# One opening block, later constants made inside the first attention, and call lists of their own for the passes without an output stage

## What is computed

```python
# layer 0, with shift/scale/gate vectors from silu(c0) @ wmod0 (6 x 256 per sample)
h = _layernorm(x) * (1 + scale_a) + shift_a
x = x + gate_a * attention(h)        # 16 heads of 16, causal, layer-normed q and k, exact softmax
h = _layernorm(x) * (1 + scale_b) + shift_b
u = silu(h @ w1.T * s1) * (h @ w2.T * s2)
u = gelu(u @ h1.T * sh1); u = gelu(u @ h2.T * sh2)
x = x + gate_b * (u @ w3.T * s3)
# layer 1, with vectors from silu(c1) @ wmod1
x = x + gate_a * selective_scan_block(h)   # in_proj, dt/B/C projection, scan over 512 steps, 16 states
x = x + gate_b * (mx_quantize(h) @ mx_quantize(weight).T + bias)
```

## Time and profile before

| | us |
|---|---|
| median of 3 runs | 4080.57 (4078.65 to 4083.61) |
| profiled execution, its own time | 4077.96 |
| its span in the trace | 4076.2 |
| TensorE busy | 3502.1 (86%) |
| VectorE busy | 3318.9 (81%) |
| ScalarE busy | 2577.2 (63%) |
| GpSimd busy | 2721.2 (67%) |

### The profile page before, as it was taken

How to read it: one execution, slowest core, us unless ns; L and a number is a source line. 1 busy time by engine, 2 the same in 40 slices (tenths; PEclk the granted TensorE clock), 3 DMA queues, 4 the chain that set the end, 5 groups by cost and what they waited for, 6 DMA issues and landing times. The chain is left out here.

```text
span 4076.2 us, 49893 instructions
## 1 busy us (share of the span) xinstructions
PE 3502.1 (86%) x16757; PEld 2034.7 (50%) x16757; DVE 3318.9 (81%) x3665; ACT 2577.2 (63%) x3716; POOL 2721.2 (67%) x1957
## 2 busy tenths in 40 slices
PE   5488888989898998989897898989889898989876
PEld 3154553637355463736455373645546373644522
DVE  3513687989888898989887898988989898988997
ACT  2345666766676766766676676666667676667652
POOL 0031676958677685968766695877768696776892
PEclk9599999999999999999999999999999999999888
DMA  3520110303021020302112030301103030211100
GB/s 136 183 88 32 58 63 8 118 1 109 16 67 59 28 98 6 116 4 91 35 53 74 6 119 1 99 27 57 69 21 104 1 109 16 78 47 42 68 1 11
DMA packets 66249, 236.01 MB, mean 58 GB/s; under 512 B 9120, under 2 KB 9760, under 8 KB 65568
## 3 DMA queue, kind: packets, MB, share of 16 engines
q1 hardware_dynamic: 63648, 223.81, 16.3%
q10 hardware_dynamic: 2304, 8.39, 0.5%
HBM read 212.25 MB, written 19.92 MB: 57 GB/s over the span
## 5 line engine op out<-in xcount | busy, mean ns | idle before, releaser
L672 POOL TENSOR_TENSOR kept<-kept,hb 128x512 f32<-128x512 f32 x600 | 757.5, 1294 | 20.2 <-DVE hb L1989 19.6
L1980 DVE TENSOR_TENSOR_SCAN hb<-ps,hb 128x512 f32<-128x512 f32 x600 | 697.8, 1206 | 17.7 <-ACT ps L1404 13.1
L938 PE MATMUL ps<-hid_bhi,wring 128*128 128x512 f32 x1408 | 560.9, 398 | 16.0 <-DVE ln_s L2007 16.0
L938 PE MATMUL ps<-hid_blo,wring 128*128 128x512 f32 x1408 | 554.1, 394 | 0.0
L1404 ACT ACTIVATE ps<-kept,a_neg 128x512 f32<-128x512 f32 x600 | 403.3, 695 | 188.1 <-DVE hb L1980 188.1
L938 PE MATMUL ps<-hid_ahi,wring 128*128 128x512 f32 x1280 | 515.2, 402 | 4.9 <-DVE h_ln L2007 4.4
L633 POOL TENSOR_SCALAR_AFFINE_SELECT room<-room 128x512 f32<-128x512 f32 x256 | 224.3, 893 | 431.3 <-ACT room L1628 429.4
L938 PE MATMUL ps<-hid_alo,wring 128*128 128x512 f32 x1280 | 505.0, 395 | 0.0
L2055 DVE TENSOR_REDUCE room<-ps 128x4 f32<-128x2048 f32 (+3 forms) x256 | 375.1, 1486 | 118.1 <-PE ps L1132 118.1
L640 POOL TENSOR_TENSOR kept<-kept,hb 128x1024 f32<-128x1024 f32 x112 | 288.9, 2590 | 249.0 <-DVE hb L1924 181.1
L1628 ACT ACTIVATE room<-ps 128x2048 f32<-128x2048 f32 (+1 forms) x192 | 305.3, 1590 | 205.4 <-PE ps L1158 178.5
(11 more groups left out here) (319 smaller groups left out, 7680.1 us busy)
## 6 DMA issues: line engine op xcount, KB each, us to landing
wring<-w_hi SPq DMA_DIRECT2D x352, 512.0 KB, 3.3
kept<-in_wffn SPq DMA_DIRECT2D x22, 512.0 KB, 4.4
w_hi<-wring SPq DMA_DIRECT2D x22, 512.0 KB, 3.6
xn<-in_x_fm SPq DMA_DIRECT2D x17, 512.0 KB, 3.2
out_fm<-xc ACTq DMA_DIRECT2D x15, 512.0 KB, 2.7
room<-in_wmod SPq DMA_DIRECT2D x2, 1536.0 KB, 7.8
win<-in_win SPq DMA_DIRECT2D x1, 1024.0 KB, 8.7
wqk<-in_wqk SPq DMA_DIRECT2D x1, 512.0 KB, 5.7
```

What stands on the lines that cost most here:

```text
L672: pool.tensor_tensor(acc[:, m, :], acc[:, m, :], hb[:, s % 8, :], ALU.add).then_inc(acc_done, 1)
L938: mm = pe.matmul(bank(bk), w, x, start=(k == 0 and i == 0), stop=(k == K - 1 and i == 1))
L1980: dve.tensor_tensor_scan(hb[:, s % 8, :], bank(2 + m % 2), hb[:, s % 8, :], 0.0, ALU.mult, ALU.add).then_inc(scanned, 1)
```

## The change

- The setup block, the two memset blocks and the pass of number -1 become one block, `opening`. SP loads 16 tensors in it: the two c inputs, `mean_mat`, sample 0, the modulation matrix of layer 0, and what attention needs. The layer norm of sample 0 starts when its own two loads are there, and its variance product stands between the fourth and the fifth of the 12 groups of modulation products.
- The other 14 constants are loaded by SP in the first pass, one behind each stage load from tile 3 to tile 16. The modulation of layer 1 is made in the first pass (`later_pe`, `later_act`, `later_dve`). The quantisation of the last weight is made in the feed pass (`feed_dve`, `feed_pe`, `feed_act`).
- POOL, PE, ACT and DVE have a second list, for passes with `fin` false: the first pass, the feed pass and pass 1. For passes with `fin` true the lists are as they were, call for call. The second lists hold the same calls in another order, with the splitting steps at other places.

```diff
-        with nc.Block() as block:
-            n_set = len(SETUP_LOADS) + 10
...
+        def opening():
+            n_opening = 11
+
+            with nc.Block() as block:
+                @block.sync
+                def _(sp):
+                    sp.dma_start(c_in[:, 0, :], a["c0"]).then_inc(c_loaded, 16)
+                    sp.dma_start(c_in[:, 1, :], a["c1"]).then_inc(c_loaded, 16)
+                    sp.dma_start(whole(mean_mat), a["mean_mat"]).then_inc(x_loaded, 16)
+                    sp.dma_start(xn[:, :, :], a["x_fm"][0]).then_inc(x_loaded, 16)
+                    sp.dma_start(wm[0], a["wmod0"]).then_inc(mod_loaded, 16)
...
+                @block.scalar
+                def _(act):
+                    act.wait_ge(c_loaded, 32)
+                    act.activation(c_s, c_in, ACT.Silu).then_inc(set_act, 1)
+                    act.preload_act_table_set(LN_EXP)
+                    act.wait_ge(next_cent, 1)
+                    act.activation(qk_sq, ln_x[:, :, :], ACT.Square).then_inc(next_sq, 1)
...
+                    act.wait_ge(set_pe, 1)
+                    copy_modulation(act, 0, 0)
+                    act.wait_ge(next_norm, 1)
+                    act.wait_ge(set_dve, 2)
+                    for c in range(DC):
+                        act.activation(ln_x[:, c, :], ln_x[:, c, :], ACT.Identity, bias=mod[0][:, SA + c, 0:1],
+                                       scale=mod[0][:, CA + c, 0:1]).then_inc(att_in, 1)
...
+                @block.tensor
+                def _(pe):
+                    pe.wait_ge(x_loaded, 32)
+                    for c in range(DC):
+                        mm = pe.matmul(bank(6), mean_mat[:, :], xn[:, c, :], start=(c == 0), stop=(c == DC - 1))
+                    mm.then_inc(next_mean_done, 1)
+                    pe.wait_ge(mod_loaded, 16)
+                    pe.wait_ge(set_act, 1)
                     for m in range(6 * DC):
...
+                        mm = modulation(pe, 0, m, 0)
+                        if m == 3:
+                            pe.wait_ge(next_sq, 1)
+                            for c in range(DC):
+                                vv = pe.matmul(bank(7), mean_mat[:, :], qk_sq[:, c, :], start=(c == 0), stop=(c == DC - 1))
+                            vv.then_inc(next_var_done, 1)
...
+                @block.vector
+                def _(dve):
+                    dve.wait_ge(next_mean_done, 1)
+                    dve.tensor_tensor(ln_x[:, :, :], xn[:, :, :], bcast_c(bank(6)), ALU.subtract).then_inc(next_cent, 1)
+                    dve.wait_ge(next_rstd_ready, 1)
+                    dve.tensor_tensor(ln_x[:, :, :], ln_x[:, :, :], bcast_c(bank(7)), ALU.mult).then_inc(next_norm, 1)
+                    dve.wait_ge(set_act, 2)
+                    scales_of(dve, 0)
+                    gates_of(dve, 0, 2)
+
+                    dve.wait_ge(loaded, 16 * n_opening)
...
+        def later_pe(pe):
+            pe.wait_ge(loaded, 16 * N_LATER)
+            for m in range(6 * DC):
+                mm = modulation(pe, 1, m, 5)
+            mm.then_inc(set_pe, 1)
...
+        def feed_dve(dve):
+            for i in range(QN):
+                quant(dve, ffw, DC * D // QB, set_dve, 12, i)
...
                     sp.dma_start(stage[:, t % 3, :], a["wffn"][t]).then_inc(stage_loaded[t % 3], 16)
+                    if 3 <= t < 3 + N_LATER:
+                        to, name = LATER_LOADS[t - 3]
+                        sp.dma_start(to, a[name]).then_inc(loaded, 16)
...
+            if fin:
...
+            else:
+                split(0, 1)
+                square(0)
+                square(1)
...
-        run([Pass(-1, False, False, False, False, True, False, ())])
+        opening()
         turn_over()
         run([Pass(0, True, False, False, False, False, True, ())])
```

1946 lines of the change are left out of this document (1252 added, 694 removed).

## The result

The changed kernel took 4033.5 us in the median of 4 runs (4028.5 to 4041.4), the kernel before 4079.9 beside it: 0.9887 of its time, 95% interval 0.9872 to 0.9902. The forecast was 4024, the range 4004 to 4049. So the direction and the range held, and the gain is 46 us instead of 56. The profiled execution had a span of 4033.4 us (before 4076.2) in a run of 4035.1 us; between the two profiled executions the gain is 42.8 us.

A forecast was written before the change was run, and what follows sets the result against it. Before 453 us chains of waits bound the kernel, after that nearly full engines (DVE, PE). Opening -35.5, first pass -22, feed pass +5.1 and pass 1 -4 sum to -56.4, so 4024.2 us, range 4004 to 4049.

The forecast's parts named there:

- Opening, forecast -35.5: Opening: the first pass starts at 30.6 us instead of 66.1, a gain of 35.5 us.
- the 48 products: Opening: modulation matmuls on PE at the lower clock level, 16 in 3.4 us and 32 in 6.9.
- the result of -40: Opening: if sustained work raised the clock, some 4.5 us shorter, at -40; set aside in favour of the trace.
- the bound of -39: Opening: the largest gain allowed, -39 us, if the clock rises for the products.
- First pass, forecast -22: First pass: -28.4 us from reordered lists, +6.1 for the added modulation work; bounds -34 and -8.
- The walk: First pass: tile and attention chains stepped through from its start, putting scores_turned(2, 1) at 99.6 instead of 127.95, -28.4 us.
- the added loads: First pass: 14 loads, 3.8 MB, 9.5 us of transfer; the two large ones put at 0 cost.
- The rival with all 9.5: First pass: added loads queue ahead of the stage loads and take 9.5 us back, kernel at 4034; 12%.
- Feed pass, forecast +5.1: Feed pass: quantisation first on DVE delays the centring chain by 5.8 us, earlier rounding returns 0.7; bounds +4 and +7.
- Pass 1, forecast -4: Pass 1: an earlier exponential, and head-state work moved into an attention wait; -4 us, bounds -9 and +6.
- Steady passes, forecast 0: The 14 steady passes: lists kept, so no change unless the change does something to the clock.
- rival 4: Steady passes: a shifted start lowers the clock, each losing up to 3.7 us, 51 in all, kernel at 4075; 3%.

The follow-up runs named there:

- first_old: Changed kernel with its first pass running the kernel before's call lists, later constants ahead of scores(3,2), exp_probs(3,1) and weigh(3); 4062.1 us, 0.9962 of the kernel before.
- loads_late: Changed kernel with its 14 later loads issued behind the last tile instead of behind stage loads 3 to 16; 4036.1 us, 0.9896 of the kernel before.
- all_moved: Changed kernel joining quant_late, z_late, loads_late (wmod1 left early), opening_wqk, later_early and four extra opening matmuls on a zeroed tile; 4014.4 us, 0.9843.
- later_early: Changed kernel with later_pe's products in three parts, ahead of scores(1,1), scores(1,2) and scores(2,1) of the first pass; 4031.7 us, 0.9887 of the kernel before.
- quant_late: Changed kernel with VectorE's late weight quantisation moved from the feed pass's front to behind gate_up(7); 0.9883 of the kernel before.
- z_late: Changed kernel with two ScalarE calls exchanged in the new list, invert_sums(3) ahead of copy_z(0); 0.9883 of the kernel before.
- opening_wqk: Changed kernel with VectorE's preparation of wqk ahead of the scales and gates in the opening; 0.9885 of the kernel before.

## Why the prediction was right, and where it was off

**Opening, forecast -35.5, measured -37.6 in the profiled execution and -39 as a mean of nine traces.** The steps are the forecast's, and DVE's `wqk` preparation is the last as forecast. The term that was mis-sized is the 48 products, put at 10.3 us. I had taken the low level of the 96 products before for a property of such small matmuls and set aside the result of -40 with the clock raised. Nine traces show both: a start of 28.4 to 30.5 (-36 to -38) with the 32 products at 6.85 us, and of 24.4 to 25.6 (-41 to -42) with 3.7 to 4.2, past the bound of -39. Where all 48 products were at the lower level, the start (30.2 and 30.5 us) is the forecast's 30.6: the steps were right, and the gain beyond it is the clock's. The Trainium skill (TensorE: Matmul & The Clock Gate, Part 1: The HAM clock gate) says sustained work raises the clock; five traces of nine agree, in two the level rose and fell again ahead of the 32 products, and in two it stayed low through all 48.

**First pass, forecast -22, measured -15.6.** The walk was right in mechanism and nearly in size: first_old gives 27.8 for the lists, the walk 28.4. But its landmark `scores_turned(2, 1)` came at 104.0 and not 99.6. Of these 4.4 us the added loads, which I put at 0, are the likely 3: loads_late and all_moved show 3 in the tile chain, behind the 1 MB load, where I had counted 4 us of slack, and nothing behind the 1.5 MB load. The rival with all 9.5 was too large. The Trainium skill (DMA: Bandwidth & Descriptors, Queues, rings and completion order) says that on each DMA engine a queue's descriptors are consumed in ring order; the 7.3 us of tile 9's load against 3.4 in loads_late fit it. And `later_pe` was put at 5.5, since PE waits there anyway; it cost 7.0 to 7.3, and the pass's tail grew by 8.3 us instead of 6.1. Moved away, it leaves the pass some 6 us shorter (later_early).

**Feed pass, forecast +5.1, measured +6.1.** The step held as written; quant_late takes 6.8 of it back. Missing was that PE, idle for 6.83 us, went on mostly at its lower level (3.43 instead of 1.95).

**Pass 1, forecast -4, measured +1.2.** This step failed, in both halves. The moves that I counted happened. I had the second head state's scan shorten the second half, as the half where DVE is full; DVE's busy time there fell by 3.1 us and the half by 0.2 (114.76 to 114.57), so DVE's work did not set its length. In the attention half the last exponential came 108.1 us behind the start and not earlier than before (106.8), with PE busy 87.2 us instead of 80.8 for the same matmuls, at a granted clock of 0.87 against 0.94; in z_late, at 0.90, it came at 104.7. The forecast had no term for such a loss here; the order that brings calls ahead met more of the lower level in each of its traces, and why is open. The misplaced `copy_z(0)` ahead of `invert_sums(3)` is worth 1.1 us of the loss.

**Steady passes, forecast 0, measured +3.1.** This is not of the change: quant_late and opening_wqk, with the same code there, have 3507.9 and 3508.0 us, before has 3508.5. The traces reach from 3507.9 to 3515.2. The slower ones have single passes of 234.5 us instead of 232. The row of such a pass in z_late, and below it the same pass in quant_late:

```profile
1343.30:1577.80 234.50, 211.31 (x1033) 122.96 (x1033) 204.78 (x225) 158.22 (x229) 171.22 (x122) 0.99 0.16 55
```
```profile
1332.60:1565.00 232.40, 209.61 (x1033) 122.81 (x1033) 203.58 (x225) 158.37 (x229) 171.86 (x122) 0.99 0.17 55
```

PE is busy 1.7 us longer for the same count of matmuls, which is what more of the lower level would do. That is rival 4 in small: 7 us in all, where it was priced at 51. Steady passes are some 232 us apart, before and after; the prediction's 242 was misread.

**The sum.** -37.6 - 15.6 + 6.1 + 1.2 + 3.1 = -42.8, which is 4033.4 - 4076.2. Against the forecast's -56.4 that is 13.6 less: 6.4 from the first pass, 5.2 from pass 1, 3.1 from the steady passes, 1.0 from the feed pass, and 2.1 the other way from the opening.

## What to carry to other kernels

- Where every engine runs a list, a step that frees a buffer must not stand behind a call whose input needs that buffer's user. But weigh the whole order: of the 27.8 us the place with the longest wait was worth 4.
- Work that leaves a prologue has to land in a wait, and it can be cut to fit: 48 products of 7.4 us in one piece cost 7 us, in three pieces in front of waiting score products next to nothing. At the head of a pass whose first steps are one chain it costs all of its length.
- A large load in the queue of a latency-bound chain costs by its slack: a 1 MB load 3.5 us ahead of the next stage load cost 3 us, a 1.5 MB load 7.5 us ahead nothing.
- Read small edits by the edited stage, and within it from the last event that the edit can't touch: z_late's stage was 4.4 us shorter, and only 1.1 of that came behind the last exponential, where the edit is.

## What the runs showed of the hardware

Until it first changes, the granted clock does not tell TensorE's level at the start of a program. In z_late the record is 1.00 over the whole opening. The row of 18 to 22 us there, with PE busy throughout, holds 20 matmul records; 32 of them took 6.85 us:

```profile
18.00:22.00 4.00, 4.00 (x20) 4.00 (x20) 1.22 (x1) 0.25 (x1) 0.00 (x0) 1.00 0.00 0
```

In the changed kernel the record is 1.00 over the mean's products too (3.78 us, the lower level), but from its fall at 13.0 us on it agrees with them. The same products there, with the record at 0.50:

```profile
17.00:21.00 4.00, 4.00 (x21) 4.00 (x20) 0.53 (x1) 0.00 (x0) 0.00 (x0) 0.50 0.00 0
```

Matmuls of one kind are the measure there: four of 512 columns take 3.76 us at the lower level (1.2 GHz) and 1.98 at the higher (2.4 GHz). Which of them the same code meets in its first 20 us varied from trace to trace and moved the start of the first pass by 6 us.
